# Transposing a cross-attention step's probabilities in two interleaved 64-row halves, one head to a half and a PSUM bank

## What is computed

```
q = (x @ Wq + bq).reshape(B, N, H, hd).transpose(0, 2, 1, 3)     # B 8, N 64, H 16, hd 32
kv = (ctx @ Wkv + bkv).reshape(B, K, 2, H, hd).transpose(2, 0, 3, 1, 4)   # K 1601
k, v = (kv[0], kv[1])
attn = jnp.einsum('bhnd,bhkd->bhnk', q * SCALE, k)
attn = jax.nn.softmax(attn, axis=-1)
out = jnp.einsum('bhnk,bhkd->bhnd', attn, v)
```

## Time and profile before

| | before |
|---|---|
| median of 3 runs | 1443.15 us (1438.57 to 1444.59) |
| the profiled execution | 1441.31 us, span 1439.4 us |
| mean granted TensorE clock over the span | 0.976 |
| PE busy, matmul / weight load | 93% / 81% |
| DVE, ACT, POOL busy | 66%, 53%, 8% |
| DMA, mean | 102 GB/s |

### The profile page before, as it was taken

One profiled execution on the slowest core, in us unless ns is written; L12 is line 12 of the kernel. 1 busy time (PEld: TensorE's weight loads), 2 busy tenths in 40 slices (PEclk: granted clock), 3 DMA queues, 4 the chain that ended last, 5 costly groups with the idle time before them and its releaser, 6 DMA issues.

```text
span 1439.4 us, 22011 instructions
## 1 busy us (share of the span) xinstructions
PE 1340.1 (93%) x7407; PEld 1163.4 (81%) x7408; DVE 945.1 (66%) x1506; ACT 765.6 (53%) x1328; POOL 109.9 (8%) x79
## 2 busy tenths in 40 slices
PE   5999999999999999999999999956999699999995
PEld 4788988898899899898898888844888577877774
DVE  3666666666667666666666666658579746577872
ACT  3455555565556556555555555543332426578771
POOL 0000000000000000000000000074523120000001
PEclk9999999999999999999999999968999799999998
DMA  5121011110110101112101100572446357399983
GB/s 190 71 71 32 27 44 44 33 44 30 47 44 22 35 28 57 29 33 58 29 26 47 48 26 16 104 183 48 78 160 252 128 198 255 126 324 345 342 293 95
DMA packets 129443, 146.14 MB, mean 102 GB/s; under 512 B 66408, under 2 KB 69864, under 8 KB 129392
## 3 DMA queue, kind: packets, MB, share of 16 engines
q1 hardware_dynamic: 128128, 141.49, 32.1%
q0 software_dynamic: 1280, 4.20, 0.9%
HBM read 125.02 MB, written 20.12 MB: 101 GB/s over the span
## 4 chain that ended last, share of the span: by engine, by line
PE 69%; DVE 14%; issue 7%; DMA 5%; ACT 4%; SPq 1%; DVEq 0%; POOL 0%; ACTq 0%; POOLq 0%
PE ps_scores L151 12%; PE ps_scores L153 12%; PE ps_scores L152 12%; PE ps_out L779 6%; PE ps_turn L767 5%; PE ps_scores L756 5%; DMA b1rows<-b_parts 3%; PE ps_turn L665 2%; DVE wu_lo L1905 2%; DVE stat L621 2%; PE ps_scores L2011 2%; PE ps_scores L2009 2%; PE ps_scores L2010 2%; DVE Ks L531 2%; DVE PT L609 1%
## 5 line engine op out<-in xcount | busy, mean ns | idle before, releaser
L531 DVE SCALAR_TENSOR_TENSOR Ks<-ps_scores,bkc,Ks 64x384 fp32r<-64x384 f32 (+2 forms) x254 | 160.6, 632 | 147.2 <-ACT Ks L415 143.7
L151 PE MATMUL ps_scores<-cT_hi,Wkv_hi 128*128 128x384 f32 (+2 forms) x508 | 184.3, 363 | 6.4 <-DVE Wkv_lo L553 6.4
L493 ACT ACTIVATE Pr<-ps_scores,stat 128x705 f32<-128x705 f32 (+1 forms) x128 | 119.7, 935 | 115.9 <-DVE stat L621 115.9
L153 PE MATMUL ps_scores<-cT_hi,Wkv_lo 128*128 128x384 f32 (+2 forms) x508 | 175.0, 344 | 0.0
L152 PE MATMUL ps_scores<-cT_lo,Wkv_hi 128*128 128x384 f32 (+2 forms) x508 | 174.6, 344 | 0.0
L415 ACT ACTIVATE Ks<-ps_scores,bkc 64x384 fp32r<-64x384 f32 (+2 forms) x254 | 150.0, 590 | 41.8 <-PE ps_scores L153 40.2
L151 PE MATMUL ps_scores<-Wkv_hi,cT_hi 128*128 128x512 f32 (+1 forms) x412 | 170.1, 413 | 0.4 <-DVE Ks L531 0.4
L480 ACT CAST PT<-ps_turn 128x512 fp32r<-128x512 f32 (+2 forms) x256 | 110.4, 484 | 110.8 <-PE ps_turn L767 110.0
L537 DVE TENSOR_TENSOR Vs<-ps_scores,Vs 128x512 fp32r<-128x512 f32 (+1 forms) x103 | 71.2, 691 | 148.7 <-ACT Vs L419 148.2
L153 PE MATMUL ps_scores<-Wkv_hi,cT_lo 128*128 128x512 f32 (+1 forms) x412 | 161.8, 393 | 0.0
L152 PE MATMUL ps_scores<-Wkv_lo,cT_hi 128*128 128x512 f32 (+1 forms) x412 | 161.1, 391 | 0.0
(11 more groups left out here) (357 smaller groups left out, 2512.7 us busy)
## 6 DMA issues: line engine op xcount, KB each, us to landing
wu_raw<-in_L_ffn_W_dram SPq DMA_DIRECT2D x64, 1024.0 KB, 6.7
raw<-in_ctx_dram SPq DMA_DIRECT2D x16, 768.0 KB, 4.5
raw<-in_ctx_dram SPq DMA_DIRECT2D x8, 1024.0 KB, 5.2
raw<-in_ctx_dram SPq DMA_DIRECT2D x8, 512.0 KB
sorted_x<-zeros SPq DMA_DIRECT2D x1, 4096.0 KB, 15.2
sorted_out<-zeros SPq DMA_DIRECT2D x1, 4096.0 KB, 25.7
o_heads<-U SPq DMA_DIRECT2D x56, 64.0 KB, 1.7
oA<-o_heads SPq DMA_DIRECT2D x8, 448.0 KB, 9.1
```

Of the source, the lines that this page charges most:

```text
L151: nc.tensor.matmul(out_ap, sh, mh, start=(i == 0), stop=False)
L153: last = nc.tensor.matmul(out_ap, sl, mh, start=False, stop=(i == len(pairs) - 1))
L493: nc.scalar.activation(Pr[:, i % 2, 0:VALID[c]], S_cols(c, 0, VALID[c]), ACT.Exp, bias=stat[:, 0, c, i:i + 1], accum_out=stat[:, 1, c, i:i ...
L531: ins = nc.vector.scalar_tensor_tensor(out=Ks[c][64:128, j, o:o + wide], in0=acc[64 * h:64 * h + 64, 0:wide], scalar=bkc[:, j:j + 1], in1= ...
```

## The change

PE no longer turns the 128 partitions of a tile at once. For each tile it makes two transposes, one of partitions 0 to 63 and one of partitions 64 to 127, each with 64 columns of the identity to stream, and their outputs go to two banks: head 0's turns all lie in `ps_turn0`, head 1's in `ps_turn1`, 64 columns for each tile. The two kinds alternate. Both banks have to be free before the first one (one wait instead of two), and a semaphore that nothing waits for, `turn_begun`, is raised by an instruction between the waits and the turns. Both groups' `turned` now come with the last tile's two transposes.

ACT and DVE take each bank with one instruction for each head, over all tiles, the 65-row tile among them with its full 128 partitions (the rows beyond 65 are never used); the target in `PT` is 64 columns wide for each tile.

The diff, with ACT's copy in the second piece and DVE's in the third (its removed lines are ACT's, with a subtraction in place of the copy):

```diff
-        def prob_groups(c):
-            return (range(0, 4), range(4, CHUNK[c][1]))
+        def turned_probs(c, h):
+            n = CHUNK[c][1]
+            return bank(P_BANKS[h])[:, 0:S * n].rearrange("p (t r) -> p t r", r=S)
+
+        def kept_probs(c, h, part):
+            return PT[:, 0:CHUNK[c][1], part, S * h:S * (h + 1)]
...
-                        tiles = prob_groups(c)[q]
-                        full = [t for t in tiles if tile_rows(CHUNK[c][0] + t) == P]
                         act.wait_ge(sem("turned"), turn0 + n + 1)
-                        ins = nc.scalar.copy(PT[:, full[0]:full[-1] + 1, 0, :],
-                                             acc[:, 0:P * len(full)].rearrange("p (t r) -> p t r", r=P))
-                        if len(full) < len(tiles):
-                            ins = nc.scalar.copy(PT[0:TAIL, tiles[-1], 0, :],
-                                                 acc[0:TAIL, P * len(full):P * len(tiles)])
-                        ins.then_inc(sem("turn_hi"), 1)
+                        nc.scalar.copy(kept_probs(c, q, 0), turned_probs(c, q)).then_inc(sem("turn_hi"), 1)
...
+                        nc.vector.tensor_tensor(kept_probs(c, q, 1), turned_probs(c, q), f32(kept_probs(c, q, 0)),
+                                                ALU.subtract).then_inc(sem("turn_lo"), 1)
...
-                    def turn_probs(i, q):
-                        if q == 0:
-                            pe.wait_ge(sem("p_exp"), pair0 + i + 1)
-                        pe.wait_ge(sem("turn_lo"), turn0 + (q - 1 if i == 1 else turn_of_probs(i - 1, q, ctx) + 1))
-                        tiles = prob_groups(c)[q]
-                        for t in tiles:
-                            M, at = tile_rows(CHUNK[c][0] + t), (t - tiles[0]) * P
-                            ins = nc.tensor.matmul(bank(P_BANKS[q])[0:M, at:at + P],
-                                                   Pr[:, (i - 1) % 2, t * P:t * P + M], ident[:, :],
-                                                   is_transpose=True, start=True, stop=True)
-                        ins.then_inc(sem("turned"), 1)
+                    def turn_probs(i):
+                        pe.wait_ge(sem("p_exp"), pair0 + i + 1)
+                        pe.wait_ge(sem("turn_lo"), turn0 + (0 if i == 1 else turn_of_probs(i - 1, 1, ctx) + 1))
+                        pe.sem_inc(sem("turn_begun"), 1)
+                        last = CHUNK[c][1] - 1
+                        for t in range(last + 1):
+                            M = tile_rows(CHUNK[c][0] + t)
+                            for h in range(2):
+                                rows = slice(64 * h, 64 * h + 64)
+                                ins = nc.tensor.matmul(bank(P_BANKS[h])[0:M, S * t:S * (t + 1)],
+                                                       Pr[rows, (i - 1) % 2, t * P:t * P + M], ident[rows, rows],
+                                                       is_transpose=True, start=True, stop=True)
+                                if t == last:
+                                    ins.then_inc(sem("turned"), 1)
...
-                            turn_probs(i, 0)
-                            turn_probs(i, 1)
+                            turn_probs(i)
```

More of the change, by code:

```diff
@@ L475, in probs_hi @@
                         n = turn_of_probs(i, q, ctx)
-                        acc = bank(P_BANKS[q])
-                        tiles = prob_groups(c)[q]
-                        full = [t for t in tiles if tile_rows(CHUNK[c][0] + t) == P]
                         act.wait_ge(sem("turned"), turn0 + n + 1)
-                        ins = nc.scalar.copy(PT[:, full[0]:full[-1] + 1, 0, :],
-                                             acc[:, 0:P * len(full)].rearrange("p (t r) -> p t r", r=P))
-                        if len(full) < len(tiles):
-                            ins = nc.scalar.copy(PT[0:TAIL, tiles[-1], 0, :],
-                                                 acc[0:TAIL, P * len(full):P * len(tiles)])
-                        ins.then_inc(sem("turn_hi"), 1)
+                        nc.scalar.copy(kept_probs(c, q, 0), turned_probs(c, q)).then_inc(sem("turn_hi"), 1)
                     for i in range(STEPS):
@@ L604, in probs_lo @@
                         n = turn_of_probs(i, q, ctx)
-                        acc = bank(P_BANKS[q])
-                        tiles = prob_groups(c)[q]
-                        full = [t for t in tiles if tile_rows(CHUNK[c][0] + t) == P]
                         dve.wait_ge(sem("turn_hi"), turn0 + n + 1)
-                        ins = nc.vector.tensor_tensor(PT[:, full[0]:full[-1] + 1, 1, :],
-                                                      acc[:, 0:P * len(full)].rearrange("p (t r) -> p t r", r=P),
-                                                      f32(PT[:, full[0]:full[-1] + 1, 0, :]), ALU.subtract)
-                        if len(full) < len(tiles):
-                            ins = nc.vector.tensor_tensor(PT[0:TAIL, tiles[-1], 1, :],
-                                                          acc[0:TAIL, P * len(full):P * len(tiles)],
-                                                          f32(PT[0:TAIL, tiles[-1], 0, :]), ALU.subtract)
-                        ins.then_inc(sem("turn_lo"), 1)
+                        nc.vector.tensor_tensor(kept_probs(c, q, 1), turned_probs(c, q), f32(kept_probs(c, q, 0)),
+                                                ALU.subtract).then_inc(sem("turn_lo"), 1)
                     for i in range(STEPS):
```

## The result

| | before | changed |
|---|---|---|
| median | 1442.39 us (12 runs, 1438.57 to 1445.57) | 1449.01 us (12 runs, 1444.81 to 1455.41) |
| profiled execution | 1441.31 us, span 1439.4 us | 1444.91 us, span 1443.2 us |
| mean granted clock | 0.976 | 0.973 |

The ratio is 1.0051, with a 95% interval of 1.0032 to 1.0070: slower by 0.5%, where 1.7% faster was forecast. The slowest runs lie 10.6 us above the fastest, before 7.0 us.

A forecast was written before the change was run, and what follows sets the result against it. PE was taken as the bound, busy 830.0 of 840 us. The terms summed as 1441.3 - 38.3 + 5.9 - 1 + 9.4 = 1417.3 us, some 1.7% less; likeliest range 1404 to 1432, whole range up to 1466.

The forecast's parts named there:

- Term 1: PE's 832 turns: a side-by-side pair of 64-row transposes takes 0.064 us instead of 0.110, a gain of 38.3 us.
- loads in series: Rival, PE's turns: both halves' weight loads go one after another, 0.128 us a pair, 1461 us in all; chance 0.20.
- nothing side by side: Rival, PE's turns: streams follow streams, 0.110 us a pair as now, 1441 to about 1447 us; chance 0.12.
- Term 3: PE's array changing from 128 rows to 64 and back, 256 times: taken as 0, bound from above 0.162 us each.
- term 2: End of the turns: the next piece's 0.11 us first load has only 0.064 to hide in, 5.9 us lost.
- Term 4: ACT's and DVE's copies of the turns: one 65-row instruction less on DVE in chunk 1, 1 us gained.
- Term 5: In 37 steps with one piece, PE's gain turns into waiting for DVE: 9.4 us back at most, taken whole.
- Term 6: Before PE's turns: one wait for both banks and the extra `turn_begun` instruction cost 0, or 3.2 us if uncovered.
- changing form drains PE: Rival: each of 256 changes of the array's form empties PE, up to 0.162 us, 1437 to 1458 us; chance 0.20.

The follow-up runs named there:

- the version written out: The changed kernel with PE's loop over the seven batches written out, other engines keeping theirs: 1440.60 us (12 runs), ratio to before 0.9993.

## Why the prediction was wrong

*Term 1, the turns themselves: right.* 0.062 us a pair against the 0.064 taken. In the step shown, loads and matmuls of the two halves start within 6 ns of each other. The Trainium skill (TensorEngine Tiling (Array Packing), Key Properties) says that different tiles can load weights and run matmuls in parallel; the trace agrees. The rivals with loads in series, 0.128, and with nothing side by side, 0.110, are both out. The gain is 832 x 0.048 = 40 us.

*Term 3, the change of form: the step that failed.* It was put at 0, "the nearest row's value", with 0.162 each kept for a rival. Measured are 0.09 us of empty array at each change, and behind it a weight load with nothing before it to hide in: 0.06 us going in, 0.11 coming out. Of the latter, term 2 already counted 0.046. That is 0.15 + 0.15 = 0.30 us a step, 128 x 0.30 = 38 us, just under the 0.162 x 2. The Trainium skill (TensorEngine Tiling (Array Packing), Key Properties) says that changing the tiling mode drains TensorE; the traces agree, with the 0.09 us. The row that was taken as nearest changed columns and not rows, and at half the clock; it was the wrong neighbour. That the bound from above, 0.162, came so near is partly luck: it was the price of the emptying alone, which is 0.09, and it had no bare load in it.

*Term 2: the mechanism right*, but it went with term 3: with the array empty, nothing of L151's load is hidden, so the whole 0.11 shows.

*Term 4*: PE's waits for DVE's copies were 5.6 us before and are 3.9 (L602), 4.4 in the version written out, so 1.2 to 1.7 us gained, 1 predicted. "Down by some 10 us each" was too much: DVE and ACT have 4 and 5 us less, and the term's own numbers for DVE, 1.08 us down to 1.0 in 64 steps, give 5.

*Term 5, what DVE gives back*: 9.4 us were taken off a gain that wasn't there. With nothing gained, DVE had nothing to give back, and no run here tested it. The waits were also read too widely: of the 10.0 us "where DVE is late", 4.4 are for ACT's exponential in the second step of a batch.

*Term 6*: the waits and the extra instruction stood in no wait of PE and cost nothing that was seen. But instructions have a length too, which was not counted: 104 more transposes in a pass of the loop, each with its load, are the 208 more instructions, and through the late passes and the half clock behind them they cost the 8.4 us between the looped and the written-out version. No term and no rival had this; it is the difference between "no change" and "slower".

The sum as it should have been: 1441.3 - 40 + 5.9 + 38 - 1.7 = 1443.5, and with the 6.9 us of that profile's late passes 1450.4. Its own time was 1444.9, because the stages behind the batches happened to take 5.7 us less than before; the median, 1449.0, is nearer to the sum. The rival "changing form drains PE" had a chance of 0.20 and prices of 1437 at half and 1458 in full; the measured 0.15 a change is nearly the full price and by that rival's own sum 1417 + 38 = 1455, of which 9.4 are term 5's. It was the right mechanism, and it had less than half the weight of the forecast (0.48).

## What to carry to other kernels

Count how often a kernel changes the form of TensorE's array, and put a drain (0.09 us here) and a bare weight load (0.06 to 0.11 us) on each change: side-by-side halves pay only in rows longer than that, here beyond seven pairs. When an estimate needs a price that no row shows, ask what the mechanism would have to do, and give its bound from above the weight that it has by that, not the value of a row which differs in the very thing that is asked. And a change that puts more instructions in a loop should be tried once with the loop written out. A mean clock of 1.00 over a long stretch does not say that the clock never fell: look behind each idle time of PE.

## What the runs showed of the hardware

- Two 64-row halves of the array, with outputs in different banks, work truly side by side: loads 2 to 6 ns apart in the step shown, a pair each 0.062 us, and halves of one kind in a row no sooner (0.062 each).
- Between matmuls of 128 rows and matmuls of 64 the array runs empty: 0.09 us between the end of the last stream, by its pace from start to start, and the next load, both ways, beside large matmuls and between small transposes alike.
- PE's loop restarts without delay at 1467, 1579 and 1665 instructions; at 1711 and 1809 code is brought again all six times that the loop goes back, and PE's first instruction is some 2 us late; at 1675 it depends on the kernel and the execution. Straight code of the same work is brought in time.
- Behind 2.5 us of PE idle the granted clock fell from 1.00 to 0.50 for the next stretch of full work (427.8 to 431.2 us), and 384-column matmuls went from 0.17 to 0.32 us apart; behind idle times near 2 us it fell in five of twelve cases.
